# Three orders of work in an attention layer rewritten, and the next layer's projection as three fp32r products

## The reference

```python
# layer 0 (8 heads of 32 channels)
keys, queries, values = conv1x1(x, Wk, bk), conv1x1(x, Wq, bq), conv1x1(x, Wv, bv)
context = einsum('nhkp,nhvp->nhkv', softmax(keys, places), values)
x1 = conv1x1(einsum('nhkv,nhkp->nhvp', context, softmax(queries, channels)), Wp, bp) + x
# layer 1 (32 + 32 heads of 8 channels)
qkv = einsum('oc,bchw->bohw', w_qkv, x1)                    # 768 channels
agg = grouped1x1(depthwise5x5(qkv, w_dw), w_pw)
q, k, v = relu(q), relu(k), v of concat([qkv, agg])
att = (v1 k^T) q, each divided by its last row               # v1 = [v, 1]
out = einsum('oc,bchw->bohw', w_proj, att)
result = batchnorm(out over images and places) + x1
```

## Time and profile before

| | |
|---|---|
| time, median of 3 runs | 2342.22 us (2340.42 to 2342.7) |
| the profiled execution | 2342.65 us, its span 2340.9 us |
| granted TensorE clock, mean | 0.957 |
| busy: TensorE, VectorE, ScalarE, GpSimd | 2131.3, 1383.4, 833.8, 581.7 us |
| projection L726: 1536 instructions (two per product) | 389.8 us |
| convolution L745: 4608 instructions in 384 steps | 619.2 us, 1.61 a step |
| output products L853: 24 pairs of chunks | 127.9 + 127.8 us, 10.7 a pair |
| ScalarE's copies L936 and L955, mean | 401 and 412 ns |
| VectorE's product of a share L1149, mean | 1457 ns |
| DMA moved | 448 MB, 191 GB/s on average |

### The profile page before, as it was taken

The page is one execution under the profiler, slowest core; times in us unless marked ns, Lnnn a source line. Parts: engine busy times, 40 slices in busy tenths (PEclk is TensorE's granted clock), DMA queues, the critical chain, the costliest instruction groups (busy, mean ns, idle before and its releaser), DMA issues. The chain is left out here.

```text
span 2340.9 us, 31988 instructions
## 1 busy us (share of the span) xinstructions
PE 2131.3 (91%) x12680; PEld 1511.7 (65%) x12680; DVE 1383.4 (59%) x2042; ACT 833.8 (36%) x1807; POOL 581.7 (25%) x495
## 2 busy tenths in 40 slices
PE   6999999999699899999999999999999999999810
PEld 6888888889566466666666666666666666665500
DVE  4667766767307838556565683864756558380452
ACT  4434444343244233332342333333334233333142
POOL 2233122321221422222232332222223233212000
PEclk9999999999899899999999999999999999999865
DMA  2201222020376864865686586487568658646578
GB/s 106 81 38 44 82 82 81 1 81 41 126 259 224 286 217 160 289 230 210 226 280 210 182 282 220 168 289 235 194 249 272 212 186 274 225 174 222 232 325 360
DMA packets 137412, 448.15 MB, mean 191 GB/s; under 512 B 6960, under 2 KB 105904, under 8 KB 119216
## 3 DMA queue, kind: packets, MB, share of 16 engines
q1 hardware_dynamic: 136112, 427.24, 51.4%
q0 software_dynamic: 1152, 18.87, 1.9%
HBM read 271.30 MB, written 174.78 MB: 191 GB/s over the span
## 5 line engine op out<-in xcount | busy, mean ns | idle before, releaser
L745 PE MATMUL cv<-work,wc 128*64 128x288 f32 x4608 | 619.2, 413 | 15.5 <-DMA work<-scratch_padded 8.9
L1091 POOL TENSOR_TENSOR wc<-taps 128x512 f32<-128x512 f32 x288 | 369.2, 1310 | 798.4 <-PE cv L745 788.5
L745 PEld LDWEIGHTS cv<-work,wc 128*64 128x64 f32 x4608 | 306.6, 136 | 260.3 <-issue 39.3
L726 PE MATMUL pj<-x,wqkv 128*128 128x288 f32 x1536 | 389.8, 410 | 19.7 <-DMA x<-scratch_x 19.7
L726 PEld LDWEIGHTS pj<-x,wqkv 128*128 128x128 f32 x1536 | 288.9, 191 | 113.6 <-issue 39.2
L1149 DVE SCALAR_TENSOR_TENSOR spun<-work,spun 128x1152 f32<-128x1152 f32 x240 | 348.5, 1457 | 0.0
L1143 DVE STREAM_SHUFFLE spun<-work 128x1152 f32<-128x1152 f32 x240 | 345.7, 1447 | 0.1
L955 ACT ACTIVATE work<-cv 128x288 f32<-128x288 f32 x384 | 158.3, 412 | 507.3 <-PE cv L745 492.0
L936 ACT COPY work<-pj 128x288 f32<-128x288 f32 x384 | 154.0, 401 | 289.0 <-PE pj L726 288.4
L408 POOL TENSOR_TENSOR qs<-qs,qrc 128x512 f32<-128x512 f32 x72 | 75.3, 1051 | 428.3 <-DVE qrc L458 428.3
L1143 DVE LOAD_MASK_SELECT spun<-work x240 | 3.3, 14 | 284.4 <-DMA work<-scratch_phases 275.9
(11 more groups left out here) (112 smaller groups left out, 3056.6 us busy)
## 6 DMA issues: line engine op xcount, KB each, us to landing
work<-scratch_padded SPq DMA_DIRECT2D x48, 2599.5 KB, 10.6
scratch_padded<-work SPq DMA_DIRECT2D x48, 1300.0 KB, 6.9
scratch_phases<-work SPq DMA_DIRECT2D x96, 576.0 KB, 5.1
work<-scratch_phases SPq DMA_DIRECT2D x64, 576.0 KB, 5.2
x<-scratch_x SPq DMA_DIRECT2D x9, 2304.0 KB, 10.3
scratch_x<-xs SPq DMA_DIRECT2D x8, 2304.0 KB, 6.9
q<-scratch_phases SPq DMA_DIRECT2D x32, 576.0 KB, 5.5
xs<-in_x SPq DMA_DIRECT2D x7, 2304.0 KB, 8.8
```

The source lines that it names most:

```text
L726: mm = nc.tensor.matmul(pj[:, c % 2, :PLANE], wqkv[:, kc, u, :], x1[:, kc, c * PLANE:(c + 1) * PLANE], start=(kc == 0), stop=(kc == CT - 1))
L745: mm = nc.tensor.matmul(cv[64 * b:64 * b + 64, j % 2, :PLANE], wc[:, 2 * j + b, dy].rearrange("p c o -> p (c o)"), window, start=(dy == 0) ...
L1091: op = nc.gpsimd.tensor_tensor(wc[:, blocks, dy], taps[:, u % 2, blocks, 0:DIM].rearrange("p g (c o) -> p g c o", o=1).to_broadcast([P, HB ...
```

## The change

**In the first layer.** (1) For the first image TensorE waits piece by piece, the first low parts are made by VectorE and not by GpSimd, and the small weights are waited for after the keys. (2) The high parts of the next image are made in the groups 3 to 6 and not 5 to 8. (3) The product of context and Wp goes into two banks, with a count for each half; `mthi` and `mtlo` follow half by half; `x1_group` goes over the halves kc in its outer loop, and its first waits for a half at a time; `turn_queries` runs two groups ahead.

**In the second layer.** The projection's fp32 product becomes three fp32r products: six instructions a chunk in place of four. x1's high part `xhi` is made by ScalarE in four parts (after the convolution steps 1, 3, 5, 7 of unit 4), its low part by VectorE in the place of x1 itself, after share 6 of product 3. The weights are split at the start. To make room `rep` becomes a ring of three half units; the second half is loaded between the two layout stores of the unit before. ScalarE's wait ahead of a projection is for the store of `qpad`, not for the load back. x1 of the last image is loaded once more for the end.

**At the end.** The stores are issued by ScalarE, that of image k behind the scaling of image k + 1.

```diff
@@ phase_l0, TensorE
-            pe.wait_ge(w_in, 16 * NW)
+                    if n == 0 and m == 0:
+                        pieces = -(-(c + 1) * CHUNK // PIECE)
+                        pe.wait_ge(hi_ready, pieces)
+                        pe.wait_ge(lo_ready, pieces)
...
-                    if g == 0:
-                        pe.wait_ge(mthi_ready, (n + 1) * CT)
-                        pe.wait_ge(mtlo_ready, (n + 1) * CT)
...
-                    for m in range(CT):
-                        for kc in range(CT):
+                    for kc in range(CT):
+                        if g == 0:
+                            pe.wait_ge(mthi_ready, n * CT + kc + 1)
+                            pe.wait_ge(mtlo_ready, n * CT + kc + 1)
+                        for m in range(CT):
...
+                if n == 0:
+                    pe.wait_ge(w_in, 16 * NW)
...
-                    mm = nc.tensor.matmul(kx[:, 1, h * C:(h + 1) * C], ctxm[:, h], wp[:, h],
-                                          start=True, stop=True, skip_group_check=True)
-                mm.then_inc(m_filled, 1)
+                    nc.tensor.matmul(mbank(h), ctxm[:, h], wp[:, h],
+                                     start=True, stop=True, skip_group_check=True).then_inc(m_filled, 1)
                 for g in range(NPAIR):
-                    if 1 <= g < NPAIR - 1:
-                        turn_queries(g + 1)
+                    if g < NPAIR - 2:
+                        turn_queries(g + 2)
                     x1_group(g)
@@ phase_l0, ScalarE
-                    if nxt and 5 <= g < 5 + PIECES:
-                        if g == 5:
+                    if nxt and 3 <= g < 3 + PIECES:
+                        if g == 3:
                             wait_count(act, qv_filled, n * NPAIR)
-                        high(split_input(act, par, it), g - 5)
+                        high(split_input(act, par, it), g - 3)
@@ phase_l1, SyncE
+            def replica(i, u, h):
+
+                n = i * NU + u
+                size = HB * PADDED + ROW - 1 if h == 0 else HB * PADDED - 1
+                sp.wait_ge(padded_out[u % 2], (n // 2 + 1) * 16)
+                if 2 * n + h >= 3:
+                    sp.wait_ge(cv_filled, (n - 1) * NG + (4 if h else 0))
...
-                    lay_store(i, u)
+                    lay_store(i, u, [0])
+                    if u + 1 < NU or nxt:
+                        replica(*unit_at(i, u + 1), 1)
+                    lay_store(i, u, [1])
...
-                    if u == 3 and nxt:
+                    if u == 3:
                         sp.wait_ge(pj_filled, i * (NU * NG) + NU * NG)
-                        sp.dma_start(x1[:], dram["x1"][i + 1]).then_inc(x_in, 16)
+                        sp.dma_start(x1[:], dram["x1"][i + 1 if nxt else i]).then_inc(x_in if nxt else x_again, 16)
@@ phase_l1, TensorE
-                if u == 0:
-                    pe.wait_ge(x_in, 16 * i + 16)
                 for c in chunks:
+                    if u == 0 and c % 2 == 0:
+                        pe.wait_ge(xhi_ready, 4 * i + c // 2 + 1)
+                        pe.wait_ge(xlo_ready, 4 * i + c // 2 + 1)
...
-                        mm = nc.tensor.matmul(pj[:, c % 2, :PLANE], wqkv[:, kc, u, :],
-                                              x1[:, kc, c * PLANE:(c + 1) * PLANE],
-                                              start=(kc == 0), stop=(kc == CT - 1))
+                        high, low = (a[:, kc, c * PLANE:(c + 1) * PLANE] for a in (xhi[:], xlo[:]))
+                        nc.tensor.matmul(pj[:, c % 2, :PLANE], whi[:, kc, u, :], high, start=(kc == 0), stop=False)
+                        nc.tensor.matmul(pj[:, c % 2, :PLANE], whi[:, kc, u, :], low, start=False, stop=False)
+                        mm = nc.tensor.matmul(pj[:, c % 2, :PLANE], wlo[:, kc, u, :], high, start=False, stop=(kc == CT - 1))
@@ phase_l1, ScalarE
+            def high(i, s):
+
+                act.wait_ge(x_in, 16 * (i + 1))
+                nc.scalar.copy(x_part(xhi, s), x_part(x1, s)).then_inc(xhi_ready, 1)
...
-                    act.wait_ge(rep_in[u % 2], (NU // 2 * i + u // 2) * NREP)
+                    act.wait_ge(padded_out[u % 2], (NU // 2 * i + u // 2) * 16)
...
+                        if u == 4 and nxt and j % 2:
+                            high(i + 1, j // 2)
@@ phase_l1, VectorE
+                for s in parts:
+                    dve.wait_ge(xhi_ready, 4 * i + s + 1)
+                    nc.vector.tensor_tensor(x_part(xlo, s), x_part(x1, s), x_part(xhi, s).bitcast(F32),
+                                            ALU.subtract).then_inc(xlo_ready, 1)
...
-                    spin(i, 3, range(0, 9))
+                    spin(i, 3, range(0, 6))
+                    low(i + 1, range(4))
+                    spin(i, 3, range(6, 9))
@@ phase_out, ScalarE
+            def store_out(k):
+
+                act.wait_ge(summed, k + 1)
+                act.dma_start(dram["out"][order[k]], buffers[k % NB][0]).then_inc(store[k % NB], 16)
+
...
+                if k:
+                    store_out(k - 1)
+            store_out(NIMG - 1)
```

More of the change, by code:

```diff
@@ L425, in _ @@
             nc.vector.tensor_tensor(wlo[:], wkqv[:], whi[:].bitcast(F32), ALU.subtract).then_inc(w_lo, 1)
+            for s in range(PIECES):
+                dve.wait_ge(hi_ready, s + 1)
+                nc.vector.tensor_tensor(piece(xlo, 0, s), piece(xs, 0, s), piece(xhi, 0, s).bitcast(F32),
+                                        ALU.subtract).then_inc(lo_ready, 1)
             dve.wait_ge(w_in, 16 * NW)
@@ L512, in _, with phase_l1 @@
                     image(2 * it + par, par)
-def phase_l1(nc, dram, sem, bnst, q, x1, work, early):
+def phase_l1(nc, dram, sem, bnst, q, x1, xhi, xlo, work, early, x_again):
     with ExitStack() as ctx:
@@ L524, in ps @@
             return ctx.enter_context(nc.psum_tensor(name, shape, F32))
-        wqkv = sb("wqkv", [P, CT, NU, P])
+        whi = sb("w1hi", [P, CT, NU, P], F32R)
+        wlo = sb("w1lo", [P, CT, NU, P], F32R)
         wproj = sb("wproj", [P, 4, C])
@@ L566, in phase_l1 @@
         taps_in = (taps_in0, taps_in1)
-        rep_in, padded_out = (rep_in0, rep_in1), (padded_out0, padded_out1)
+        padded_out = (padded_out0, padded_out1)
+        rep_in = [sem(f"l1_rep_in{r}") for r in range(3)]
+        w_split, xhi_ready, xlo_ready = sem("l1_w_split"), sem("l1_xhi_ready"), sem("l1_xlo_ready")
         lay_stored, lay_done = ((lay_stored0, lay_stored1), (lay_stored2, lay_stored3)), ((lay_done0, lay_done1), (lay_done2, lay_done3))
@@ L635, in replicate @@
             def replicate(i, u):
-                n = NU // 2 * i + u // 2
-                sp.wait_ge(pj_freed, i * (NU * NG) + (u + 1) * NG)
-                wait_count(sp, rep_in[u % 2], n * NREP)
+                n = i * NU + u
+                sp.wait_ge(pj_freed, (n + 1) * NG)
+                if n >= 2:
+                    for h in range(2):
+                        sp.wait_ge(rep_in[ring(n - 2, h)], ring_at(n - 2, h))
                 sp.dma_start(dram["padded"][u % 2].rearrange("l p n -> p l n"),
@@ L695, in _ @@
             replicate(0, 0)
+            replica(0, 0, 1)
             replicate(0, 1)
@@ L919, in _ @@
         def _(act):
+            act.wait_ge(w_first, 16 * NFIRST)
+            nc.scalar.copy(whi[:], wqkv).then_inc(w_split, 1)
+            def high(i, s):
+                act.wait_ge(x_in, 16 * (i + 1))
+                nc.scalar.copy(x_part(xhi, s), x_part(x1, s)).then_inc(xhi_ready, 1)
+            for s in range(4):
+                high(0, s)
             act.wait_ge(zeroed, 1)
@@ L1130, in _, with low @@
         def _(dve):
+            dve.wait_ge(w_split, 1)
+            nc.vector.tensor_tensor(wlo[:], wqkv, whi[:].bitcast(F32), ALU.subtract).then_inc(w_split, 1)
+            def low(i, parts):
+                for s in parts:
+                    dve.wait_ge(xhi_ready, 4 * i + s + 1)
+                    nc.vector.tensor_tensor(x_part(xlo, s), x_part(x1, s), x_part(xhi, s).bitcast(F32),
+                                            ALU.subtract).then_inc(xlo_ready, 1)
+            low(0, range(4))
             def spin(i, p, share):
@@ L1259, in _ @@
                 sp.dma_start(x, dram["x1"][order[k]]).then_inc(loaded, 16)
-        @block.gpsimd
-        def _(pool):
-            for k in range(NIMG):
-                pool.wait_ge(summed, k + 1)
-                pool.dma_start(dram["out"][order[k]], buffers[k % NB][0]).then_inc(store[k % NB], 16)
-            for r in range(NB):
-                pool.wait_ge(store[r], 16 * len(range(r, NIMG, NB)))
         @block.scalar
         def _(act):
+            def store_out(k):
+                act.wait_ge(summed, k + 1)
+                act.dma_start(dram["out"][order[k]], buffers[k % NB][0]).then_inc(store[k % NB], 16)
             act.wait_ge(stat, CT + 1)
@@ L1280, in _ @@
                 last.then_inc(scaled, 1)
+                if k:
+                    store_out(k - 1)
+            store_out(NIMG - 1)
```

(2 more changed lines are left out.)

88 lines of the change are left out of this document (54 added, 34 removed).

## The result

| | before | after |
|---|---|---|
| median | 2342.46 us (2340.42 to 2343.2) | 2300.11 us (2298.37 to 2302.27) |
| the profiled execution, its span | 2342.65, 2340.9 us | 2298.37, 2296.6 us |
| granted TensorE clock, mean | 0.957 | 0.954 |

The ratio is 0.9818, with an interval from 0.9802 to 0.9834: 42 us less, where 107 were forecast and 2266 was the upper end. The direction was right and the size was not.

A forecast was written before the change was run, and what follows sets the result against it. Bounds were TensorE with stalls in the first layer, TensorE alone in the second, DMA at the end. The terms summed to -107.0 us from 2342.65, giving 2235.6; the forecast was 2236, range 2212 to 2266.

The forecast's parts named there:

- Two dates follow: Steady image: VectorE's low part (first date) and sums with mask (second) would both reach TensorE in time, 1.6 us left each.
- the ring: Second layer's half replicas: TensorE's replica waits would go, -1.1 us outside image 0; SyncE waits there for nothing not past.
- The four subtractions, 5.4 us: VectorE's low part in a steady image: 1.36 us per 1152-column subtraction, 5.4 together, plus about 0.5 of waiting.
- my first rival: VectorE becomes a steady image's bound: TensorE waits three us in each of 7 images, +21, 2257 us; chance 0.17.
- The products, 0.133 us, -59.5: Second layer's projection: six fp32r products of 0.133 us save 0.186 a chunk, -59.5 us over 320 chunks.
- products at their columns alone: Rival in the second layer's projection: fp32r products take 0.123 us each, 320 chunks give 79 us, 2217 us; chance 0.07.
- a split that doesn't pay: Rival in the second layer's projection: products take 0.173 us, 1.04 a chunk, 18 us lost, 2313 us; chance 0.03.
- First layer, -8.9 - 7.4 - 12.8 - 12 = -41.1: First layer: earlier start -8.9, high parts two groups earlier -7.4, halves and earlier queries -12.8, clock -12 us.
- The clock's 12: First layer: shorter stalls would win back most of the time lost to TensorE's lower clock, -12 us, between 0 and -16.
- Image 0, -6.1: Start of second layer and image 0: -6.1 us, between 0 and -12, with a new stall before image 1's projection.
- my fourth rival: ScalarE's queue stopped by a late x1 load, as high parts stand ahead of convolution copies: 2350 us; chance 0.02.
- End, -5: DMA-bound end: stores moved from GpSimd's to ScalarE's queue behind the next image's scaling, -5 us, between -9 and +10.

The follow-up runs named there:

- SyncE's order: Kernel after, with the lay-out load of unit 4 issued on SyncE behind the padded store and half replica of the next image's unit 0: 2243.41 us.
- the subtractions 2 us later still: Kernel after, with the statistics of the image before put ahead of the four low-part subtractions on VectorE: 2258.87 us.
- the fastest complete kernel: Kernel after, with unit 4's lay-out load behind the replica on SyncE and the four subtractions after five shares in place of six: 2235.44 us.
- the kernel before with SyncE's order: Kernel before, with only unit 4's lay-out load moved behind the next image's padded store and replica on SyncE: 2334.34 us.

## Why the prediction was wrong, and where it was right

*Two dates follow.* This is the step that failed. Of the subtractions I asked who on TensorE waits for what stands behind them, found the low part and the mask, and stopped. A third piece of work stood behind them, the statistics, and for these it is SyncE that waits, with the padded store and the next replica in its queue. I had written of the ring that SyncE "waits there for nothing that isn't past" and priced it at -1.1, from the half loads alone. What would have shown it is a view that I read for TensorE only: SyncE's own waits, with 33.1 us in six for these statistics. There was almost no slack. In SyncE's queue of the kernel before, the load was out just ahead of the store, for which the projection ended at 991.79:

```profile
990.32 1.12 SPq L668 DMA_DIRECT2D q<-scratch_phases  x2
992.32 0.37 SPq L640 DMA_DIRECT2D scratch_padded<-work  x1
```

```profile
991.79 2.41 PE L745 MATMUL cv<-work,wc 128*64 128x288 f32 x18
```

The load's two issues were through at 991.44, so no more than 0.8 us later would have cost nothing; the subtractions took 6.9, while TensorE's own date came earlier with each cheaper unit. The price was 7.5 us of wait and 1.5 of lower clock in each of six images, 54 of the 64 us missed, and putting SyncE's order right brought 57 back.

*The four subtractions, 5.4 us.* Mis-sized: 6.9 to 7.8. One that starts beside nothing on GpSimd takes 1.36, and one beside its weight operations 2.2, as 15 of the 28 ahead of the images 1 to 7 did. That was my first rival's mechanism. I had priced it at 3 us in 7 images, with TensorE waiting for the low part directly, and set 0.17 on it. As a direct wait it exists, but is small: 0.6 us in two of six images with SyncE's order, 2.5 in five with the subtractions 2 us later still. So my 1.6 us of room on the first date was nothing. The second date held: TensorE's waits for the mask are one of 0.9 us, where one of 0.8 was before. The Trainium skill, "SBUF — State Buffer", section "Who interferes with whom", has a VectorE operation with two SBUF inputs and a reading GpSimd one exclude each other for a whole instruction. I had taken the low end against it. The trace is nearer to the page: a subtraction and one weight operation, 1.36 and 1.04 alone, 2.40 in a row, come every 2.15 us.

*The products, 0.133 us, -59.5.* Right in the price of a product and nearly right in the sum. A unit took 6.39 us (6.38 forecast). A steady image is 186.14 in the fastest complete kernel and 193.93 in the kernel before with SyncE's order: 7.8, where 48 chunks x 0.186 are 8.9, and 8.1 with the 0.8 an image that I had set against them. One unit of the six gives less, the next image's unit 0: 7.31 us in the kernel after, where the others took 6.4 to 6.7, and 7.96 before. Its first copies stand on ScalarE behind the fourth high part, and TensorE waits for them. That is a part of the difference, and "nothing" for the high parts was a little too low:

```profile
931.61 1.15 ACT L970 CAST x1hi<-x 128x1152 fp32r<-128x1152 f32 x1
932.66 0.83 ACT L990 COPY work<-pj 128x288 f32<-128x288 f32 x2
```

```profile
933.21 0.37 PE L768 MATMUL pj<-x1hi,w1hi 128*128 128x288 f32 x1 [0.15 <-ACT work L990]
```

The rivals of products at their columns alone and of a split that doesn't pay are out. The 0.1225 that I worked out from the gap formula of the Trainium skill, "TensorE: Matmul & The Clock Gate", section "Back-to-back issue gap", which the page gives for an isolated product, is too low for these products in a row.

*First layer, -8.9 - 7.4 - 12.8 - 12 = -41.1.* Right: 43.8 by the run of it alone, and TensorE's first product of the second layer came 42.0 us earlier, although a high and a low part (2.6 us) now stand ahead of it. Start: 8.9 by its run. The first product is at 9.80 (9.65 forecast). Waits for ekT fell by 7.4, as forecast to the tenth; those for mtlo by 12.3 (12.8). The clock's 12 came out near 15 (43.8 less 8.9, 7.4 and 12.3). But that term belongs to neither part: each alone got 6 to 12 of it.

*Image 0, -6.1.* Mis-sized: from the first product of the second layer to the first convolution of image 1 it is 177.65 us in place of 180.55, -2.9. The stalls for replicas (4.81 us in the earlier trace rows, and one of 2.71) went, the one for weights grew from 6.37 to 11.1 us, and two others came. The stall that I had foretold before image 1's projection is there with 2.96 us. The one for ScalarE's copies (3.7 us) is my fourth rival on a small scale: high waits in its queue for the x1 load.

*End, -5.* Mis-sized: -1.7. The last store went out 9.5 us after the last load had landed, as said (about 10), and from the last load on the DMA engines were busy for 0.66 of the time, up from 0.49, in the row below; the rest of the idle time stayed, for the last image's scaling, sum and store stand in a row as before.

```profile
2279.64:2296.60 16.96, 0.00 (x0) 0.00 (x0) 4.96 (x1) 4.50 (x2) 0.00 (x0) 0.50 0.66 278
```

*The range* could not hold the result, for its upper end was drawn from the prices of routes that I had listed. VectorE's delay had a chance in it at 3 us an image; one more queue on its way made it 9. With the order on SyncE put right and the subtractions a share earlier, the kernel takes 2235.44 against my 2236. That it agrees is luck in part: the share earlier gave 8 us that were not in my sum, and they stand in for what image 0 and the end gave less than forecast.

## What to carry over

When work is added to an engine, list everything that stands behind it there and for each piece every engine and queue that waits for it; a DMA queue's own waits are a view to read beside those of the engine that bounds the kernel. In a DMA queue put a transfer whose condition comes late behind those that the bound engine needs next. And when a change that shortens the bound engine's work moves the time by nothing, look in the new trace for the one wait per round that has grown: here a whole gain of 7 us an image sat in it.

## What the runs showed of the hardware

- A 128x1152 subtraction on VectorE with both inputs in SBUF takes 1.36 us alone and 2.2 beside GpSimd's 128x512 multiplications; such a multiplication took 1.98 in place of about 1.04, and the two came in turn every 2.15 us.
- A small space for GpSimd's DMA descriptors (256) turned first stores 4.9 us apart into ones 12 to 18 us apart, with idle time that the trace ascribes to nothing, and made the end 5 us longer.
- After each wait of about 7.5 us TensorE's next twelve products took 3.15 us in place of 1.68, at a granted clock of 0.50, and the granted clock over a steady image was 0.98 in place of 1.00. In the first layer, with two waits of about 2 us in a row, shortening either one to 0.9 us or less brought the clock from 0.96 to 0.99.
